# A gated delta rule on one core: from looped head pairs to one unrolled two-phase pipeline

## What is computed

```python
qkvz = x @ W_qkvz                      # q, k, v, z of each head
q, k, v = silu(causal_conv4(q, k, v))  # depthwise, 4 taps
q, k = l2norm(q) * 128 ** -0.5, l2norm(k)
g = cumsum(gate per chunk); decay = tril(exp(g_i - g_j))
tri = tril((k * beta) @ k.T * decay, -1)
Tm = inverse(eye + tri)                # 64 x 64, per chunk
v_new, k_cum = Tm @ (v * beta), Tm @ (k * beta * exp(g))
def step(S, chunk):                    # 8 chunks of a sequence, in order
    attn = (q @ k.T) * decay
    v_n = v_new - k_cum @ S
    out = (q * exp(g)) @ S + attn @ v_n
    S = S * exp(g_last) + (k * exp(g_last - g)).T @ v_n
y = rmsnorm(out) * norm_weight * silu(z); x = layernorm(x + y @ W_out)
```

## Time and profile before

| | us |
|---|---|
| median of 3 runs | 3685.12 (3682.16 to 3687.61) |
| profiled execution | 3688.41 |
| its span, first to last instruction | 3686.7 |
| TensorE busy in it | 3110.8 |
| VectorE busy in it | 2405.8 |

### The profile page before, as it was taken

How to read it: one execution, slowest core, us unless ns; L and a number is a source line. 1 busy time by engine, 2 the same in 40 slices (tenths; PEclk the granted TensorE clock), 3 DMA queues, 4 the chain that set the end, 5 groups by cost and what they waited for, 6 DMA issues and landing times. The chain is left out here.

```text
span 3686.7 us, 86810 instructions
## 1 busy us (share of the span) xinstructions
PE 3110.8 (84%) x32443; PEld 2201.8 (60%) x32443; DVE 2405.8 (65%) x5179; ACT 1354.5 (37%) x4204; POOL 1024.4 (28%) x1623
## 2 busy tenths in 40 slices
PE   7999996599778888888888888888888888888598
PEld 3444442366556666666666666666666666666465
DVE  4666664788636766676665765775676666766466
ACT  2344332233333433343343433443343334333254
POOL 3455544178511122112211211221122111211011
PEclk8999997799869999999999999999999999998799
DMA  2111111000010001000100000010000100000000
GB/s 77 32 33 33 30 34 36 7 1 1 13 27 22 14 16 30 14 15 16 29 15 16 21 22 16 15 29 16 15 14 16 30 14 15 29 18 2 24 18 29
DMA packets 93930, 78.90 MB, mean 21 GB/s; under 512 B 54992, under 2 KB 68320, under 8 KB 93664
## 3 DMA queue, kind: packets, MB, share of 16 engines
q1 hardware_dynamic: 93664, 75.18, 7.5%
HBM read 57.70 MB, written 4.85 MB: 17 GB/s over the span
## 5 line engine op out<-in xcount | busy, mean ns | idle before, releaser
L1394 DVE SCALAR_TENSOR_TENSOR gd_Y<-gd_bk,gd_cwh,gd_Y 128x511 f32<-128x511 f32 (+2 forms) x576 | 403.6, 743 | 77.8 <-ACT gd_Y L1287 75.4
L1562 PE MATMUL gd_bk<-gd_xT,gd_wh 128*128 128x512 f32 x768 | 417.7, 648 | 1.2 <-DMA gd_wh<-in_L_attn_W_qkvz 1.2
L1464 DVE COPY_PREDICATED gd_U<-gd_mU,gd_bk 128x256 f32<-128x256 int32 x320 | 142.7, 446 | 253.5 <-PE gd_bk L1646 177.5
L390 DVE TENSOR_REDUCE at_nm<-at_ring 128x2 f32<-128x256 f32 (+3 forms) x256 | 199.3, 821 | 148.0 <-PE at_ring L531 148.0
L1486 DVE SCALAR_TENSOR_TENSOR gd_V<-gd_bk,gd_cneg,gd_VV 64x128 f32<-64x128 f32 x512 | 161.3, 348 | 187.2 <-PE gd_bk L1675 186.2
L1630 PE MATMUL gd_bk<-gd_L,gd_NT 64*64 64x64 f32 x5120 | 208.4, 226 | 85.1 <-DVE gd_L L1466 78.2
L1356 ACT COPY gd_O<-gd_bk 64x128 f32<-64x128 f32 x512 | 125.6, 260 | 397.8 <-PE gd_bk L1675 397.0
L1630 PEld LDWEIGHTS gd_bk<-gd_L,gd_NT 64*64 64x64 f32 x5120 | 180.1, 139 | 134.1 <-issue 131.9
L1336 ACT COPY gd_ZS<-gd_bk 128x256 f32<-128x256 f32 x320 | 118.5, 373 | 381.6 <-PE gd_bk L1630 375.4
L1641 PE MATMUL gd_bk<-gd_U,gd_ZS 64*64 64x64 f32 x5120 | 229.7, 229 | 23.7 <-ACT gd_ZS L1336 12.4
L1680 PE MATMUL gd_bk<-gd_V,gd_KK 64*128 64x128 f32 x1024 | 203.9, 316 | 48.0 <-DVE gd_V L1486 46.8
(11 more groups left out here) (352 smaller groups left out, 6871.7 us busy)
## 6 DMA issues: line engine op xcount, KB each, us to landing
gd_wh<-in_L_attn_W_qkvz SPq DMA_DIRECT2D x64, 512.0 KB, 4.5
gd_gb<-gates SPq DMA_DIRECT2D x128, 64.0 KB, 4.1
X<-in_L_attn_x SPq DMA_DIRECT2D x8, 512.0 KB, 8.6
at_QT<-at_QS SPq DMA_DIRECT2D x128, 32.0 KB, 2.0
at_KT<-at_KS SPq DMA_DIRECT2D x128, 32.0 KB, 2.0
at_OC<-at_Ob SPq DMA_DIRECT2D x128, 32.0 KB, 1.9
at_RC<-inverse SPq DMA_DIRECT2D x128, 32.0 KB, 1.8
out_x<-X SPq DMA_DIRECT2D x8, 512.0 KB, 2.9
```

Of the source, the lines that this page charges most:

```text
L390: nc.vector.tensor_reduce(nm[v % 2][:, k, c0:c0 + HS + 1:HS], set_of(s, 2 + p)[:, :, 0:n], AX.X, ALU.max).then_inc(max_done, 1)
L1394: ins = nc.vector.scalar_tensor_tensor(out, bk[e][j][:, 0:W - s], cwh[e][:, CV[j], CONVK - 1 - s:CONVK - s], out, ALU.mult, ALU.add)
L1562: ins = nc.tensor.matmul(bk[e][(0, 1, 2, 2)[j]][:, :], wh[e][:, k, WCOL[j] * DK:(WCOL[j] + 1) * DK], xT[:, k, :], start=k == 0, stop=k == ...
```

## The change

The main block of `delta_rule` is written anew, without hardware loops: waits are on constants, and table columns are read in place. The three POOL copies per head and the copy of a sequence's rows to `xs` are gone. For a run of q from -1 to 31, with f = q + 1, each engine's list has two phases:

1. Recurrence steps n = 0 to 8 of pair q, with most of the front of pair f placed between their instructions (`front_early` ahead of the state update, `front_late` behind it). Step 0 has no state product; S begins as a copy of the key product. Both heads are in the same chunk at each step (`m = n`).
2. Levels 1 to 5 of pair f, with the q projection, v and q taps, v transposes, q norms of pair f and the heads' scaling and transposes of pair q placed in them, and the output projection of a finished sequence in levels 4 and 5.

Silu is now ScalarE's own function, so the halving of weights, Tanh and VectorE's products for it are gone. The sums of squares for the norms are matmuls of the squared k and q with a column of ones; q is no longer transposed. Tiles that both phases use are doubled. In the core of the diff below, "-" lines show the old loop.

```diff
-                    nc.vector.tensor_scalar(cw[:, :, :, :].rearrange("p a b c -> p (a b c)"),
-                                            cw[:, :, :, :].rearrange("p a b c -> p (a b c)"), 0.5, None, ALU.mult)
-                    nc.vector.tensor_scalar(nw_row[:, :], nw_row[:, :], 0.5, None, ALU.mult)
...
-        def pairs(eng, body):
-            with eng.Fori(0, B - 1) as b:
-                with eng.Fori(0, HP - 1) as hp:
-                    body(b, b * HP + hp, hp * 2, (b, hp * 2 + 2), False)
...
             @block.scalar
+                def gate_out(f, e):
+                    act.wait_ge(zp_mm[e], f + 1)
+                    ge(act, h_done[e], f - 1)
+                    nc.scalar.activation(flat(zz[e][f % 2][:, :, :]), F1[e][:, :], ACT.Silu).then_inc(z_silu[e], 1)
+                def keys_out(f, e):
+                    act.wait_ge(k_conv[e], f + 1)
+                    ge(act, gq_mm[e], f)
+                    ge(act, kt_mm[e], f)
+                    nc.scalar.activation(kT[e][:, :], YK[e][:, :], ACT.Silu).then_inc(k_silu[e], 1)
+                    act.wait_ge(k_silu[e], f + 1)
+                    ge(act, nq_mm[e], f)
+                    nc.scalar.activation(SQ[e][:, :], kT[e][:, :], ACT.Square).then_inc(k_sq[e], 1)
...
+                def front(f, n):
+                    if n in (0, 1):
+                        keys_first(f, n)
+                    if n in (1, 2):
+                        gate_out(f, n - 1)
+                    if n == 2:
+                        decays(f, 0)
+                        decays(f, 1)
+                    if n in (3, 4):
+                        keys_out(f, n - 3)
+                    if n in (4, 5):
+                        key_norms(f, n - 4)
+                    if n in (7, 8):
+                        values_first(f, n - 7)
...
+                    for n in range(NCH + 1):
+                        for e in E2:
+                            m = n
+                            if has(q) and 1 <= m < NCH:
+                                c, t = m % CPT, m // CPT
+                                act.wait_ge(p1_mm[e], q * RS + m)
+                                ge(act, ht_mm[e], q)
+                                nc.scalar.copy(O[e][rows(c), t, :], A_[e][rows(1 - c), 0:DK]).then_inc(o1_done[e], 1)
+                        if has(q) and n >= 2 and n % 2 == 0:
+                            squares(q, 0, n // 2 - 1)
+                        if has(q) and n >= 2 and n % 2 == 0:
+                            squares(q, 1, n // 2 - 1)
+                        if has(f):
+                            front(f, n)
...
             @block.vector
+                def front_early(f, n):
+                    if n in (1, 2, 3):
+                        for i in range(n * 2 - 2, n * 2 - 1):
+                            keys_tap(f, i // 3, i % 3 + 1)
+                    if n == 8:
+                        lower(f, 1)
+                def front_late(f, n):
+                    if n in (1, 2, 3):
+                        i = n * 2 - 1
+                        keys_tap(f, i // 3, i % 3 + 1)
+                    if n in (5, 6):
+                        keys_scaled(f, n - 5)
+                    if n == 7:
+                        lower(f, 0)
+                    if n == 8:
+                        first_level(f, 0)
+                        first_level(f, 1)
...
             @block.tensor
+                def key_norms(f, e):
+                    pe.wait_ge(k_sq[e], f + 1)
+                    pe.wait_ge(z_silu[e], f + 1)
+                    for t in range(TPS):
+                        last = nc.tensor.matmul(F1[e][:, t:t + 1], SQ[e][:, t * P:(t + 1) * P], ones[:, 0:1], start=True, stop=True)
+                    last.then_inc(nk_mm[e], 1)
...
+                def front_early(f, n):
+                    if n in (0, 1):
+                        keys_in(f, n)
+                    if n in (4, 5):
+                        keys_across(f, n - 4)
+                    if n == 7:
+                        values_in(f, 1)
+                    if n == 8:
+                        lower_across(f, 0)
+                def front_late(f, n):
+                    if n in (0, 1):
+                        gate_in(f, n)
+                    if n in (3, 4):
+                        key_norms(f, n - 3)
+                    if n in (4, 5):
+                        key_gram(f, n - 4)
+                    if n == 6:
+                        values_in(f, 0)
+                    if n == 8:
+                        lower_across(f, 1)
...
+                                if m == 0:
+                                    pe.wait_ge(vnc_done[e], q + 1)
+                                    pe.wait_ge(kc_done[e], q + 1)
+                                    moving = VV[e][rows(c), t, :]
+                                else:
+                                    pe.wait_ge(w_done[e], q * RS + m)
+                                    pe.wait_ge(o1_done[e], q * RS + m)
+                                    moving = V2[e][rows(c), t, :]
+                                nc.tensor.matmul(A_[e][:, DK:2 * DK], KK[e][q % 2][rows(c), t, :], moving, start=True, stop=True).then_inc(ds_mm[e], 1)
```

More of the change, by code:

```diff
@@ L1068, in _ @@
                     last.then_inc(gpe, 1)
[L1073 to L1086, removed]
@@ new lines, in delta_rule, with ge, has, seq @@
+        PAIRS = B * HP
+        RS = NCH - 1
+        Wq4 = W_qkvz.rearrange("(c p) n -> p c n", p=P)
+        gates4 = gates.rearrange("(b t h) n -> b h t n", b=B, h=H)
+        def ge(eng, s, n):
+            if n > 0:
+                eng.wait_ge(s, n)
+        def has(q):
+            return 0 <= q < PAIRS
+        def seq(q):
+            return q // HP
+        def head(q, e):
+            return q % HP * 2 + e
+        def column(f, q, e, t):
+            return tab[:, f, seq(q) * TPS + t, head(q, e):head(q, e) + 1]
@@ L1328, in pair, with first_tap, keys_first @@
-                def pair(b, it, h0, nxt, last):
-                    if last and nxt:
-                        load_x(nxt[0])
+                def first_tap(out, bank_, j, f, e, done):
+                    nc.scalar.activation(out[:, :], bank_[:, :], ACT.Copy, scale=cw[:, j, head(f, e), CONVK - 1:CONVK]).then_inc(done, 1)
+                def keys_first(f, e):
+                    act.wait_ge(kp_mm[e], f + 1)
+                    ge(act, v_silu[e], f)
+                    first_tap(YK[e], F0[e], K_, f, e, k0_done[e])
@@ new lines, in decays, with heads_out @@
+                def decays(f, e):
+                    act.wait_ge(gbm_done[e], f + 1)
+                    for t in range(TPS):
+                        last = nc.scalar.activation(gb[e][f % 2][:, t, :], gb[e][f % 2][:, t, :], ACT.Exp, bias=column(G_, f, e, t))
+                    last.then_inc(e_done[e], 1)
+                def heads_out(q, e):
+                    act.wait_ge(ht_mm[e], q + 1)
+                    ge(act, op_mm, seq(q) * TPS)
+                    nc.scalar.copy(hT[:, head(q, e), :], B_[e][:, :]).then_inc(ht_out[e], 1)
@@ L1375, in _ @@
-                x_out(0)
-                for j, e in ((K_, 0), (K_, 1), (Q_, 0)):
-                    tap0(0, j, e)
-                front(0, lambda: None)
-                pairs(act, pair)
+                            if has(f):
+                                act.wait_ge(z_mm[e], f * (LEVELS - 1) + l)
+                                nc.scalar.copy(ZS[e][:, :, :], chunks(A_[e])).then_inc(zs_done[e], 1)
+                        if l == 1 and has(f):
+                            queries_first(f, 0)
+                            queries_first(f, 1)
@@ new lines, in _ @@
+                        if l == 5 and ends_seq(f) and has(f + 1):
+                            act.wait_ge(xt_mm, DC * (seq(f) + 1) + 1)
+                            nc.scalar.copy(xT[:, 0, :], B_[0][:, :]).then_inc(xt_act, 1)
+                    if has(f):
+                        for e in E2:
+                            act.wait_ge(kc_mm[e], f + 1)
+                            for c in range(CPT):
+                                last = nc.scalar.copy(PQ[e][f % 2][:, :, c, c, :], chunks((A_[e], F1[e])[c]))
+                            last.then_inc(kc_done[e], 1)
@@ L1549, in _ @@
+                statistics(B - 1)
+                normalize(B - 1)
             @block.tensor
             def _(pe):
[L1551 to L1565 removed]
@@ L1711, in pair @@
-                    if nxt:
-                        front(it + 1, heads_out)
-                    else:
-                        heads_out()
-                x_in(0)
-                pe.wait_ge(xt_out, DC)
-                for j in range(2):
-                    for e in E2:
-                        for k in range(DC):
-                            project(0, j, e, k)
-                front(0, lambda: None)
-                pairs(pe, pair)
+                                    last = nc.tensor.matmul((A_[e], F1[e])[c][:, t * CK:(t + 1) * CK], KE[e][rows(c), t, :], U[e][rows(c), t, :],
```

(1 more changed line is left out.)

938 lines of the change are left out of this document (468 added, 470 removed).

## The result

| | before | after |
|---|---|---|
| median, us | 3683.64 (3681.40 to 3687.61, 4 runs) | 3887.82 (3874.42 to 3892.96, 4 runs) |
| ratio | 1 | 1.0547 [1.0519, 1.0576] |
| profiled execution, its span | 3688.41, 3686.7 | 3874.42, 3872.7 |

What follows compares the result with a forecast made beforehand. No single engine bounds the kernel; each third of a pair has its own limit. Pairs at 70.0 us, 24 x 70.0 + 7 x 87.5 = 2292.5 against 2255.5, +37, -3: +34, so 3720 us; range 3595 to 3800.

Steps and rivals of the forecast that it cites:

- The clock: Recurrence steps 3, 4 and perhaps 5: TensorE, short of work, falls to 1.2 GHz; +3.0 us a pair, bounds 0 and +7.
- step 3: Recurrence: ScalarE's queue of copies, squares, gate, two table loads, exponentials and silu is the chain; the step takes 6.5 us.
- about 3.4 us: TensorE's work in line with the chain at low clock (two norms, a gram, state products, output product), which doubles.
- +7 bound: Upper bound per pair if the clock stays low through steps 3 to 8, as in the last pair before the change.
- The much slower rival: Clock stays low through the recurrence: 74 us a pair, 3844 us in all; chance 0.11.
- The step list: Times of recurrence steps 0 to 8, sum 37.0 us, with the level phase's 30.0: 67.0 a pair at full clock.
- Table loads: ScalarE alternates Silu and Exp, so each pair pays two loads of 1.28 us, 2.6 us, inside the recurrence.
- The dearer switch: Rival: each table load may first drain ScalarE's pipe, 79 us more than the forecast, 3799 us; chance 0.04.
- The wait in step 3: Sign: step 3's ds product released by ScalarE's copy of O, 3 to 5 us late; key_norms released by Square.
- Ends of sequences: Seven pairs crossing sequences: 17.5 us on top of a pair instead of 21.8, so 87.5 against 89.6.
- Start and tail: Before the first and after the last recurrence: one state product and a memset less, about -3 us in all.
- The faster rival: Granted clock stays at its upper level: pair 67.0 us, 3626 us in all; chance 0.38.

## Why the prediction was wrong

**The step that failed is "The clock".** The prediction saw that TensorE would fall to its lower level in step 3 and took +3.0 us a pair. Measured is 75.8 against 68.7 for a pair without low clock (the mean of 68.3, 68.3 and 69.4, useless products included, so 7.1 is what the clock cost at least). At the first two pairs the forecast nearly held: 71.7 is 3.4 above 68.3, with the lower level in parts of steps 3, 4 and the levels, 13.7 us in all. Later it lasted to the end of step 6 in 17 of the 31 pairs. The term that was too small is the "about 3.4 us" of work in line with the chain: in the pair from 2068.03, steps 3 to 6 grew by 1.3, 1.8, 2.3 and 1.8 us and the rest by 1.8. The reason for staying near the lower end was that "values and projections of 1.85 us fill steps 6 and 7". They come too late: in step 5 TensorE's records fill the step at either level (2.90 of 2.90 us, 5.30 of 5.30), so it has no reserve there, and the steps grow with its slower work. The +7 bound, for a clock low through steps 3 to 8, was the right mechanism, and the measured cost lies at it. The much slower rival, 3844, was right in kind, with a chance of 0.11, and 44 us short.

Of the 152 us between the forecast of +34 and the +186 of the profiled executions, 24 x 5.8 = 139 are in the pairs within a sequence (4.1 a pair for the clock, 1.7 for a pair of 68.7 and not 67.0), 3 at the ends of sequences and 10 in start and tail.

**The step list** holds, but for step 3. State product to state product, at full clock (the kernel with useless products, from 2084.32), and in the pair of after from 2068.03:

| step | predicted | full clock | after |
|---|---|---|---|
| 1 | 5.35 | 5.6 | 5.6 |
| 2 | 3.1 | 2.6 | 2.6 |
| 3 | 6.5 | 7.6 | 8.9 |
| 4 | 4.15 | 4.4 | 6.2 |
| 5 | 2.6 | 2.9 | 5.3 |
| 6 | 4.55 | 4.1 | 5.8 |
| 7, 8, levels, 0 | 6.4 + 30.0 + 4.35 = 40.75 | 41.1 | 42.9 |
| sum | 67.0 | 68.3 | 77.3 |

In step 3 half of the missing 1.1 us is the key norms, taken at 0.5 us a head. Their row at full clock, in the timeline of the kernel with useless products, is 1.05, above the bound of a gate issue (4 x 0.24); at the lower level it is 1.87 (row of 2082.26 above):

```profile
2098.54 1.05 PE L1643 MATMUL gd_bk<-gd_ones,gd_SQ 128*128 128x1 f32 x8
```

**Table loads.** Right. 32 loads ahead of the exponentials and 32 ahead of the silu of k, 1.283 us each, both in the block of step 3. The dearer switch is refuted: the silu ends at 2075.23 + 0.60 = 2075.83 and the load starts at 2075.84; 2075.84 + 1.28 = 2077.12, the first exponential starts at 2077.14; 2079.62 + 1.28 = 2080.90, the silu at 2080.91. Against the Trainium skill, "ScalarE: Activation LUTs", section "What ACT_TABLE_LOAD costs", no drain is seen here. The Trainium skill, "ScalarE: Activation LUTs", section "Table sets: the hidden batching unit", advises to batch by set; being rid of all 64 loads (with tanh in place of silu) was worth 87 us.

**The wait in step 3.** TensorE was to be held up by the copy of O for 3 to 5 us; it waited 2.6, and the releasers are those named.

**VectorE.** 41.6 us busy in the pair from 2145.40 (a window of 74.0), predicted about 42. It is freed, and frees nothing, since TensorE and ScalarE hold the chain.

**Ends of sequences.** Predicted 87.5, measured 87.9, but by luck. In the kernel with useless products a pair at a sequence's end without low clock takes 82.5 us. An end thus adds 13.8 us to 68.7, not 17.5, and the low clock costs 5.4 there, not 3.0; the errors cancel.

**Start and tail.** -3 predicted. The first recurrence starts 4.6 us later (1130.60 against 1125.97), and from the last to the end it is 308.1 against 305.2: +7.5. This is no more than runs differ by: over the traces of the kernel after and its variants the first recurrence starts between 1124.3 and 1134.4, and the last one to the end takes 299.0 to 308.1.

**The faster rival** needed a clock that holds and gave 3626 for it. With the clock held in most pairs by useless products, the kernel measured 3678, which is a draw with the kernel before: the pair is 68.7 and not 67.0, and near the 68.9 below which the change wins. The wait for ScalarE (in step 3) and the clock are two costs: removed singly they are worth 115 and 210 us, together 291.

Left open: why the low stretch ends within step 4 in the first three pairs and behind step 6 in most others, with one list of instructions. No run was made for it.

## What to carry to other kernels

When a change thins the work beside a chain of dependent steps, price TensorE's clock as a state and not as a toll on one wait: go through each following step with TensorE at 1.2 GHz and ask whether its queue then still waits for others, or is itself the chain. If it is the chain, count these steps at up to 1.8 times their length (here 6.2, 5.3 and 5.8 us for 4.4, 2.9 and 4.1). The cheap test is a control pair: useless products where TensorE idles, and the same ones where it is busy.

## What was not expected of the hardware

- 13 useless products a pair, 6.9 us of records, made the program 210 us faster; the same 13 in a busy place made it 175 us slower.
- A TensorE whose records fill a stretch can still be granted the lower level through it: 5.30 busy of 5.30 us at 0.50, where the same step at full clock has 2.90 of 2.90. The busy share is 100% at both levels and does not show the loss.
- The lower level is not always a cost. In the front of the kernel before the granted clock was 0.92 or 1.00 with the same 20.7 us; pairs with 3.4 us of the lower level in its levels too took 1.5 longer.
- A product with one moving column and a weight load of its own is not nearly free in 32 bits: four issues took 1.05 us, and 1.87 at the lower level.
